# A graph network on one core: three attention layers rewritten around scans, and the edge MLP's first product made ahead of it

## The reference, cut to what matters

```
# middle layer, three times
xs, xd = (h @ Ws), (h @ Wd)                # heads of 32
e = leaky_relu(sum(xs*a_s)[src] + sum(xd*a_d)[dst], 0.2)
ex = exp(e - segment_max(e, dst)[dst])
out = segment_sum(xs[src] * ex / segment_sum(ex, dst)[dst], dst) + bias
# edge MLP: hidden = relu([h[src], edge_attr] @ w1 + b1), 256 wide,
# relu(hidden @ w2 + b2), summed by dst, then a linear map, before the node MLP
```

## Time and profile before

| | before |
|---|---|
| median of 3 runs | 10667.48 us (10661.7 to 10689.28) |
| the profiled execution, its own time | 10696.05 us |
| its span in the profile | 10694.3 us |
| PE, DVE, ACT, POOL busy | 5622.2, 4834.9, 1790.8, 6522.5 us |
| layer 0 / first middle layer / edge MLP, stretches of the span | 426 to 1892 / 2068 to 3440 / 6610 to 8640 us |

### The profile page before, as it was taken

How to read it: one execution, slowest core, us unless ns; L and a number is a source line. 1 busy time by engine, 2 the same in 40 slices (tenths; PEclk the granted TensorE clock), 3 DMA queues, 4 the chain that set the end, 5 groups by cost and what they waited for, 6 DMA issues and landing times. The chain is left out here.

```text
span 10694.3 us, 107517 instructions
## 1 busy us (share of the span) xinstructions
PE 5622.2 (53%) x22192; PEld 3714.7 (35%) x22192; DVE 4834.9 (45%) x11928; ACT 1790.8 (17%) x4846; POOL 6522.5 (61%) x6001
## 2 busy tenths in 40 slices
PE   6387878233333433334233334888888885333332
PEld 5133333133333333323233233444444443333332
DVE  6398989433332222222222223556565534444443
ACT  1211111211111100001000002333333331000002
POOL 2466666466666566665666665555555526888885
PEclk8688888566656556556555556999999986555555
DMA  1432324322223122222222223333333313444445
GB/s 67 120 59 56 58 56 56 78 44 46 43 45 45 38 44 46 45 45 41 45 45 46 46 46 69 88 86 91 89 92 85 90 30 31 36 36 36 36 36 95
DMA packets 705533, 611.82 MB, mean 57 GB/s; under 512 B 392917, under 2 KB 587604, under 8 KB 704308
## 3 DMA queue, kind: packets, MB, share of 16 engines
q0 software_dynamic: 332784, 513.58, 26.3%
q1 hardware_dynamic: 372676, 97.46, 4.3%
HBM read 483.12 MB, written 126.04 MB: 57 GB/s over the span
## 5 line engine op out<-in xcount | busy, mean ns | idle before, releaser
L899 POOL DMA_INDIRECT big<-table_layer,rec_L x2688 | 2658.9, 989 | 1598.8 <-issue 845.5
L970 PE MATMUL sums_L<-h,ident 128*128 128x128 f32 (+1 forms) x5376 | 1606.3, 465 | 720.7 <-DVE h L1068 301.9
L974 PE MATMUL sums_L<-carry_L,ident 128*128 128x128 f32 (+1 forms) x1792 | 679.5, 473 | 2172.6 <-DVE carry_L L1077 1438.6
L1077 DVE TENSOR_TENSOR carry_L<-sums_L,shrink_L 128x128 f32<-128x128 f32 (+1 forms) x896 | 348.1, 389 | 2841.9 <-remote 2222.7
L2061 POOL DMA_INDIRECT sums_by_source<-msg,to x896 | 1420.9, 1586 | 286.7 <-issue 227.6
L970 PEld LDWEIGHTS sums_L<-h,ident 128*128 128x128 f32 x5376 | 1092.2, 277 | 1200.3 <-issue 1175.0
L899 POOL DMA_INDIRECT big<-table_layer,idx_L x912 | 946.1, 1037 | 538.4 <-issue 307.2
L974 PEld LDWEIGHTS sums_L<-carry_L,ident 128*128 128x128 f32 x1792 | 395.2, 265 | 2359.7 <-DVE carry_L L1077 1497.4
L1611 POOL DMA_INDIRECT big<-table_layer,rec_m x900 | 859.2, 955 | 274.3 <-issue 274.3
L1661 PE MATMUL ps<-big,w 128*128 128x512 f32 x1792 | 833.5, 608 | 0.0
L924 ACT ACTIVATE big<-run_z_L 128x4 f32 (+1 forms) x900 | 194.6, 216 | 3554.4 <-DVE carry_L L1077 2257.0
(11 more groups left out here) (376 smaller groups left out, 8664.9 us busy)
## 6 DMA issues: line engine op xcount, KB each, us to landing
big<-table_layer,rec_L POOLq DMA_INDIRECT x2688
big<-table_layer,idx_L POOLq DMA_INDIRECT x912
table_layer<-xr SPq DMA_DIRECT2D x49, 296.0 KB
big<-table_layer,rec_m POOLq DMA_INDIRECT x900
sums_by_source<-msg,to POOLq DMA_INDIRECT x896
sums_by_source<-big SPq DMA_DIRECT2D x4, 3200.0 KB
q<-sums_by_source SPq DMA_DIRECT2D x28, 448.0 KB, 6.3
own_L<-own_layer SPq DMA_DIRECT2D x672, 2.0 KB
```

What stands on the lines that cost most here:

```text
L899: G.indirect_dma_start(out=g[b][:, u, s, :], out_offset=None, in_=table, in_offset=bass.IndirectOffsetOnAxis(ap=at, axis=0)).then_inc(gath ...
L970: PE.matmul(sums[b][u][:, 0:T * D], ident[:, :], prod[PROD[u]][:, s, :], start=(s == 0), stop=False, skip_group_check=True)
L974: PE.matmul(sums[b][u][:, 0:T * D], ident[:, :], carry[u % 2][:, :], start=False, stop=True, skip_group_check=True).then_inc(summed, 1)
L1077: V.tensor_tensor(carry[u % 2][:, :].rearrange("p (l c) -> p l c", c=C), before[:, 0:T * D].rearrange("p (l c) -> p l c", c=C), bc(shrink[ ...
```

## The change

1. The three middle layers are a new function, `gat`. Slots lie along the free axis, and a batch's 16 slots are summed by one VectorE scan over 4 x 33 rows of 17 elements (132 x 17 = 2244): state = shrink x state + product. The running maximum is a scan as well. TensorE makes no sums any more; it only picks own scores out of a transposed table, `own1T`, by a one-hot of the tile number. Gathers go into a ring of 4 buffers. Loops run over turns of 4 batches, 14 of them, 13 "early".
2. In each early batch 5 or 6 chunks of 128 edges (5.25 on average; a third of all edges per layer) are loaded in order, transposed and multiplied by w1's lower half, and stored to `he_d`, one row of 256 per edge. The input with windows of 4 edges becomes a plain one, `edges`.
3. The MLP gathers, in place of attributes, one window of 4 rows of `he_d` (4 KB per partition) into a ring of 4, and VectorE adds it to the gathered node rows ahead of the transposes. L1630, L1644, L1681, L1718 and L1725 go; relu1 reads PSUM. A second small fetch brings the rows' positions.
4. Tables of the middle layers are written in the sorted order, by a plain DMA from SP instead of L1335. So the gathers need positions in that order: layer 0's table gets a column with it, ScalarE copies the 16 positions of each batch, and SP stores them to `pos_d`.
5. The histogram's 13 turns are of 4 batches.

The core of the diff, without its indentation:

```diff
+def store(i, b):
+    sp.wait_ge(pos_ok[b], i + 2)
+    sp.sem_inc(gate_s, 1)
+    sp.dma_start(pos_d[:, ds((i * U + b * B) * S, B * S)], posb[b][:, :]).then_inc(pos_out[b], 16)
...
+act.wait_ge(pos_out[b], i * 16 + 16)
+A.activation(posb[b][:, :].rearrange("p (u s) -> p u s", s=S), g[b][:, :, :, A0], ACT.Copy
+             ).then_inc(pos_ok[b], 1)
...
+@block.sync
+def _(sp):
+    if more is not None and "sync_first" in more:
+        more["sync_first"](sp)
     for j in range(NT):
-        pool.wait_ge(staged, j + 1)
-        G.indirect_dma_start(out=table, out_offset=bass.IndirectOffsetOnAxis(
-            ap=nid[:, j:j + 1].bitcast(u32), axis=0), in_=st[j % STG][:, 0:width], in_offset=None
-        ).then_inc(rows_out[j % STG], 16)
+        sp.wait_ge(staged, j + 1)
+        sp.dma_start(table[j * P:(j + 1) * P, :], st[j % STG][:, 0:width]).then_inc(rows_out[j % STG], 16)
+    if more is not None and "sync_last" in more:
+        more["sync_last"](sp)
...
+def _(sp):
+    def fetch(i, b):
+        sp.dma_start(idx[b][:, :], pos_d[:, ds((i * NB + b) * SLOTS, SLOTS)]).then_inc(idx_in[b], 16)
+        sp.dma_start(jl[b][:, :, :], rec_d[:, ds((i * NB + b) * B, B), R_J:R_J + 2]
+                     ).then_inc(jl_in[b], 16)
...
+def hidden_out(i, b):
+    sp.wait_ge(he_ok, (i * NB + b) * 3 + 6)
+    sp.sem_inc(gate_s, 1)
+    sp.dma_start(edge_rows(i, b, he_d), he[b % 2][:, 0:CHUNKS[b], :]).then_inc(he_out[b % 2], 16)
+def turn(i, early):
+    for b in range(NB):
+        if early:
+            sp.wait_ge(e_turned, (i * NB + b) * 2 + 2)
+            sp.sem_inc(gate_s, 1)
+            sp.dma_start(ein[b % 2][:, 0:CHUNKS[b], :], edge_rows(i, b, edges)).then_inc(e_in[b % 2], 16)
+        sp.wait_ge(gathered[b], (i + 1) * 16 * SLOTS)
+        sp.sem_inc(gate_s, 1)
+        if early:
+            hidden_out(i, b)
+        sp.wait_ge(kept, i * NB + b + 3)
+        sp.sem_inc(gate_s, 1)
+        fetch(i + 1, b)
+for v in range(2):
...
+           allow_small_or_imprecise_dtypes=True).then_inc(wide_ok, 1)
+n = turns_of_batches(pool)
+with pool.Fori(0, n) as i:
+    for b in range(NB):
+        pool.wait_ge(idx_in[b], i * 16 + 16)
+        pool.wait_ge(used[b], i + 1)
+        pool.sem_inc(gate_p, 1)
+        for s in range(SLOTS):
+            G.indirect_dma_start(out=ring[b][:, s, :], out_offset=None, in_=tab1_d[l],
+                                 in_offset=bass.IndirectOffsetOnAxis(
+                                     ap=idx[b][:, s:s + 1].bitcast(u32), axis=0)
+                                 ).then_inc(gathered[b], 16)
...
+def hidden(i, b):
+    k = i * NB + b
+    pe.wait_ge(e_in[b % 2], (i * 2 + b // 2) * 16 + 16)
+    pe.wait_ge(eT_ok, k * 2 + 2)
+    for c in range(CHUNKS[b]):
+        last = PE.transpose(psE[c // 4][:, (c % 4) * P:(c % 4 + 1) * P], ein[b % 2][:, c, :], ident[:, :])
+        if c == 3 or c == CHUNKS[b] - 1:
+            last.then_inc(e_turned, 1)
+    for c in range(CHUNKS[b]):
+        if c % 4 == 0:
+            pe.wait_ge(eT_ok, k * 2 + c // 4 + 3)
+        if c % 2 == 0:
+            pe.wait_ge(he_ok, k * 3 + c // 2 + 1)
+        last = PE.matmul(psH[c // 2][:, (c % 2) * HID:(c % 2 + 1) * HID], eT[:, c * P:(c + 1) * P],
+                         w1[:, 1, :], start=True, stop=True)
+        if c % 2 == 1 or c == CHUNKS[b] - 1:
+            last.then_inc(he_ps, 1)
...
+def turn(i, early):
+    for b in range(NB):
+        pe.wait_ge(oh_ok, i * NB + b + 1)
+        for c in range(H):
+            last = PE.matmul(own_ps[b % 2][:, c * B:(c + 1) * B], own1T[:, c * P:(c + 1) * P],
+                             of_tile[b % 2][:, :], start=True, stop=True)
+        last.then_inc(own_ok, 1)
+        if counting and early:
+            pe.wait_ge(onehot[b % 2], i * 2 + b // 2 + 1)
+            for t in range(HSTEP):
+                last = PE.matmul(histp[:, 0:NT], oneL[b % 2][:, :, t], oneH[b % 2][:, :, t],
+                                 start=False, stop=False)
+            last.then_inc(counted[b % 2], 1)
+        if early:
+            hidden(i, b)
...
+def keep(k, b):
+    act.wait_ge(scanned, k + 1)
+    act.sem_inc(gate_a, 1)
+    for u in range(B):
+        j = act.value_load(jl[b][0:1, u, 0:1], min_val=0, max_val=NT)
+        A.activation(flat(acc1[:, ds(j, 1), :]), tot[b % 2][:, :, S * u + S], ACT.Copy)
+        last = A.drain()
+    last.then_inc(kept, 1)
+def exps(k):
+    act.wait_ge(args, k + 1)
+    A.activation(prod[:, :, :].rearrange("p (h c) s -> p h c s", h=H)[:, :, C, 1:SLOTS + 1],
+                 z[:, :, :], ACT.Exp)
+    A.activation(shrink[:, :, :].rearrange("p (h c) s -> p h c s", h=H)[:, :, :, 1:SLOTS + 1],
+                 bc(fade[:, :, :], 2, C + 1), ACT.Exp).then_inc(weighed, 1)
+def hidden(i, b):
+    k = i * NB + b
+    for v in range(2):
+        m = min(CHUNKS[b] - 4 * v, 4) * P
+        act.wait_ge(e_turned, k * 2 + v + 5)
+        A.activation(eT[:, 4 * v * P:4 * v * P + m], psE[v][:, 0:m], ACT.Copy).then_inc(eT_ok, 1)
+    act.wait_ge(he_out[b % 2], (i * 2 + b // 2) * 16 + 16)
+    for v in range(3):
+        m = min(CHUNKS[b] - 2 * v, 2)
+        act.wait_ge(he_ps, k * 3 + v + 1)
+        A.activation(flat(he[b % 2][:, 2 * v:2 * v + m, :]), psH[v][:, 0:m * HID], ACT.Copy
+                     ).then_inc(he_ok, 1)
+def turn(i, early):
+    for b in range(NB):
+        if early:
+            hidden(i, b)
+        exps(i * NB + b)
...
+def scores(i, b):
+    k = i * NB + b
+    one_hot(i + (b + 1) // NB, (b + 1) % NB)
+    V.tensor_copy(lift[:, :, 1:SLOTS + 1].rearrange("p h (u s) -> p h u s", s=S)[:, :, :, 0], bc(jl[b][:, :, 1].bitcast(fp32), 1, H))
+    V.tensor_copy(zc[:, :, 0], run_max[:, :, SLOTS])
+    dve.wait_ge(own_ok, k + 1)
+    dve.wait_ge(gathered[b], i * 16 * SLOTS + 16 * SLOTS)
+    V.tensor_tensor(z[:, :, :].rearrange("p h (u s) -> p h u s", s=S),
+                    bc(own_ps[b % 2][:, 0:H * B].rearrange("p (h u) -> p h u", h=H), 3, S),
+                    ring[b][:, :, D:A1].rearrange("p (u s) h -> p h u s", s=S), ALU.add)
+    dve.drain()
+    V.scalar_tensor_tensor(z[:, :, :], z[:, :, :], 0.2, z[:, :, :], ALU.mult, ALU.max)
+    dve.drain()
+    V.tensor_scalar(zc[:, :, 1:SLOTS + 1], z[:, :, :], LOW, None, ALU.max)
+    dve.drain()
+    V.tensor_tensor_scan(flat(run_max[:, :, :]), flat(lift[:, :, :]), flat(zc[:, :, :]), 0.0,
+                         ALU.add, ALU.max)
+    dve.drain()
+    V.tensor_tensor(fade[:, :, :], run_max[:, :, 0:SLOTS], lift[:, :, 1:SLOTS + 1], ALU.add)
+    V.tensor_tensor(z[:, :, :], z[:, :, :], run_max[:, :, 1:SLOTS + 1], ALU.subtract)
+    dve.drain()
+    V.tensor_tensor(fade[:, :, :], fade[:, :, :], run_max[:, :, 1:SLOTS + 1], ALU.subtract
+                    ).then_inc(args, 1)
+def sums(i, b):
+    k = i * NB + b
+    dve.wait_ge(weighed, k + 1)
+    p4 = prod[:, :, :].rearrange("p (h c) s -> p h c s", h=H)
+    V.tensor_copy(prod[:, :, 0], tot[1 - b % 2][:, :, SLOTS])
+    for c in range(H):
+        last = V.tensor_tensor(p4[:, c, 0:C, 1:SLOTS + 1],
+                               bc(p4[:, c, C, 1:SLOTS + 1], 1, C),
+                               ring[b][:, :, c * C:(c + 1) * C].rearrange("p s c -> p c s"),
+                               ALU.mult)
+    last.then_inc(used[b], 1)
+    dve.drain()
+    dve.wait_ge(kept, k + 1)
+    V.tensor_tensor_scan(flat(tot[b % 2]), flat(shrink[:, :, :]), flat(prod[:, :, :]), 0.0,
+                         ALU.mult, ALU.add).then_inc(scanned, 1)
...
+def turn(i, early):
+    for b in range(NB):
+        if counting and early:
+            dve.wait_ge(counted[b % 2], i * 2 + b // 2 + 1)
+            at = (i * NB + b) * HSTEP
+            V.tensor_tensor(oneL[b % 2], bc(lo[:, ds(at, HSTEP)], 1, P), wide, ALU.is_equal)
+            V.tensor_tensor(oneH[b % 2], bc(hi[:, ds(at, HSTEP)], 1, NT), wide[:, 0:NT, :],
+                            ALU.is_equal).then_inc(onehot[b % 2], 1)
+        scores(i, b)
+        sums(i, b)
...
-pool.wait_ge(rec_in[u], (i + 1) * 16)
-pool.wait_ge(turned_x, (i * U + u) * 2 + 2)
+g = i * U + u
+pool.wait_ge(rec_in[u], (i + 1) * 32)
+pool.wait_ge(turned, g * 2 + 2)
+pool.wait_ge(joined, g + U - NH + 1)
 pool.sem_inc(gate, 1)
-G.indirect_dma_start(out=ge[u][:, :, :].rearrange("p s c -> p (s c)"), out_offset=None,
-                     in_=edge_windows, in_offset=bass.IndirectOffsetOnAxis(
...
 def turn_over(i, u):
     g = i * U + u
-    pe.wait_ge(gathered[u], (i + 1) * 16 * (S + 1))
-    pe.wait_ge(eT_ok, g + 1)
-    for s in range(S):
-        last = PE.transpose(psE[u % 2][:, s * P:(s + 1) * P], ge[u][:, s, :], ident[:, :])
-    last.then_inc(turned, 1)
-    pe.wait_ge(both1, g * 2 + 2)
+    pe.wait_ge(joined, g + 1 + U)
+    pe.wait_ge(act1, g * 2 + 2)
     for f in range(2):
         for s in range(S):
-            last = PE.transpose(psX[f][:, s * P:(s + 1) * P], gx[u][:, s, f * P:(f + 1) * P],
+            last = PE.transpose(psX[u % 2][f][:, s * P:(s + 1) * P], gx[u][:, s, f * P:(f + 1) * P],
                                 ident[:, :])
```

(37 more changed lines are left out.)

452 lines of the change are left out of this document (291 added, 161 removed).

## The result

The changed kernel takes 11,401.91 us in the median of 4 runs (11,393.67 to 11,410.42), the kernel before beside it 10,664.65 us: ratio 1.0688, 95% interval 1.0669 to 1.0707. It is 737 us slower; I had forecast 12,280 us, 1613 us slower. The direction was right and the size more than twice too large.

What follows compares the result with a forecast made beforehand. Loops through all engines, plus starvation by unbroken gathers in the layers, were to bound the changed kernel: 10,696 + 1245 (layers) + 440 (MLP) - 70 (rest) = 12,311, less 29: about 12,280 us; range 10,950 to 12,900.

Steps and rivals of the forecast that it cites:

- The loop of the middle layers: Middle layers: SP's edge request waits for kept(k), so each batch runs one after the other through all engines, 26.5 us.
- the four products: Middle-layer loop, VectorE: four products at 0.68 us each, overlapping a little, within VectorE's 7.85 us.
- the exponential: Middle-layer loop: two exponentials, 64 elements 0.26 us and 2112 elements 2.3 to 2.85, taken as 2.75 together.
- GpSimd's own time: Middle layers: 16 gathers take GpSimd 20.1 us a batch, shorter than the loop, so it pauses each time.
- Starved: Middle layers: unbroken gathers stop the other engines after some 12 us; 6 us a batch, bounds 0 and 8.1.
- the forecast's layer: One middle layer: 52 x 32.5 + 56 + 62 = 1808 us against 1393, +415, three times +1245.
- the start and the late batches: Each middle layer: 62 us for the first 64 unbroken gathers, 56 for four late batches without hidden part.
- Rival 1: Middle layers: no or weak starvation, layer 1496 us, +310 in all; total 11,350, or 10,990 with MLP items at 9.3; chance 0.29.
- The rule that it took from the Trainium skill: Only the port pair VectorE and GpSimd share makes engines wait for each other; by it alone the starved term is zero.
- The MLP: Edge MLP: join of item g+2 only after reduce(g), a loop; 10.9 us an item, +440, bounds +85 and +1160.
- The rest: Other stages, mainly table writes by SP: -25 in L1in, -15 for each other; -70, bounds 0 to -130.
- the zero fill of the sums: Part of the remaining stages: the zero fills were said to stay as they were.

Runs made afterwards that it cites:

- The first run: Changed kernel with SP asking for the edges of batch k+1 once batch k's hidden product is out, not behind kept(k): 11,012.5 us (kernel before beside it 9526.1).
- the second run: Changed kernel with the MLP's join of item g+2 ahead of the reduction of item g and the mask's cast last: 10,281.9 us (kernel before beside it 9526.1).
- the seventh run: Changed kernel with both orders mended, SP's edge fetch ahead of kept and the MLP's join ahead of the reduction: 10,618.0 us, ratio 0.9932 to the kernel before.

## Why the prediction was wrong

**The loop of the middle layers: right.** Its 26.5 us are 26.7 in the timeline and 27.8 in the median. Within it the four products were taken too short (4.01 us for four times 0.68, less an overlap; they read the gathered rows at a stride of 132 elements and write into rows of 17, and which of the two costs it no run shows) and the exponential too long. The first run shows that SP's order closes it. GpSimd's own time was taken too short, 20.1 us a batch: it is busy 1149 us in the layer instead of 868, as it meets scans and products. Here the loop hides that; once the loop is open it is the bound.

**The term "Starved", 6 us a batch: this is the step that failed.** It measured 0.9 (28.5 in the mean on this chip, 27.6 on one without stops, in the second run). I had read in the earlier trace rows that an unbroken run of gathers stops whatever else is at work, and took the worst place of an old layer over to every batch of a layer with other work. In the changed second layer 368 us of unbroken gathers bring no remote wait, and the seventh run has 1446 us of them without one; what is left of the stops is four batches in 44 that are 5 to 10 us longer than the others. The term was 936 us of the forecast (three times 52 x 6) and measured about 140. With 6 replaced by 0.9 the forecast's layer is 1808-265 = 1543, and the three span 1572.8, 1537.3 and 1539.2. That it comes so close is in part luck: the loop was 1.1 us longer than forecast, and what I added for the start and the late batches made up for it.

**Rival 1, starvation none or weak, was the case.** It gave 11,350 and had 0.29. Of its grounds, that rows 4 and 5 are one place was the better one. The rule that it took from the Trainium skill (page "SBUF — State Buffer", section "Who interferes with whom") covers a gather of 5.54 us under a scan, but the part that TensorE and ScalarE never wait on anyone doesn't agree with the traces: both stand in the stops of the kernel before, ScalarE in the seventh run's MLP. Its total is close by luck too: its layers were 162 us short and its rest 95 too dear.

**The MLP: right.** +398 for +440, 10.73 us an item for 10.9, by the loop named and with the clock falling as named; the second run takes the loop away and 905 us with it (489 on a chip with stops, 2402.5 to 1913.8 in the seventh).

**The rest: too small.** -165 for -70, beyond its own bounds of 0 to -130: -83 up to the first middle layer, -84 in the three stages behind the layers, where I had -45, and +2. The table writes of the first such stage end at 1980.0 instead of 2011.7, the -25 that I had. But the next gather follows after 5.1 us instead of 56.3, since the zero fill of the sums now comes behind the index fetches on SP's queue; I had said that it stays. The four sizes together: starvation -796, the rest of the layers +23, the MLP -42 and this -95 make the 910 us between forecast and measured difference of the profiled executions.

**What hides the loss.** The old layers had 213 to 232 us each, and the old MLP 400, that a chip without stops doesn't charge. Set against such a chip the change costs 1700 us (11,217 against 9518), near what I had forecast against the other by accident: the forecast added the stops to the new kernel's layers, which lose most of them.

**Open.** What in the old layers and in the opened MLP, beside the run of gathers, brings the stops, and what differs between the chips (each was used on one occasion, one of them on two, so chip and occasion aren't told apart). Many short hand-overs among the engines fit all runs; none isolates them. Not tried: the scan with one operand in the accumulator memory. By the same section of the Trainium skill a VectorE instruction with at most one input in on-chip memory doesn't contend with GpSimd; no run here shows it.

## What to carry to other kernels

Write down each engine's program order and follow one batch around: a wait that SP or VectorE does for batch k in front of the request for batch k+1 makes a loop through all engines, and its length is the sum of the steps; here two such loops cost 198 and 905 us on chips without stops, and both together 780 us on one with them, and each went away by asking one step earlier. A wait whose releaser the trace doesn't know is not a price that can be taken over to other code: find a second place, with other work beside it, before it becomes a term. After a loop is opened, add to GpSimd's own time the VectorE instructions with two on-chip inputs that it meets, here 4.6 us a batch for one scan. And time both kernels side by side on more than one chip: the ratio here is 1.07 on one sort and about 1.18 on the other.

## What was not expected of the hardware

- One and the same kernel takes 9516.9 to 9528.9 us on one chip and 10,666.1 to 10,722.6 on another, with 1162 us (in variants of it that take as long) against 1380 in a middle layer; the changed kernel differs by under 2%, if 11,217 stands for it.
- A gather of 0.95 us lasts 5.54 when it meets a VectorE scan of 4.83 us, and 3.19 under one of 2.50.
- On a chip with stops the edge MLP with its loop opened takes 1914 us instead of 1477: ScalarE has 141 remote waits of 3.0 us in the median and up to 28.3, 532 us in all, and none on the other chip.
